# Local-attention transformer stack: queries scaled before their transposes, maximum subtracted in the score banks, one exponential per chunk, scores and weighing in halves

## The reference, cut to what matters

```
qkv = x @ Wqkv                              # 128 -> 3 * 16 heads * 64
q = l2norm(q) * q_scale;  k = l2norm(k) * k_scale
q, k = rotary(q), rotary(k)                 # times cos, plus rotated half times sin, xpos scales
# windows of 32 queries, each sees its own and the previous 32 keys, causal
sim = einsum('bhwie,bhwje->bhwij', bq, bk2) * 8.0
sim = where(mask, -max, sim)
attn = softmax(sim, -1)
out = einsum('bhwij,bhwje->bhwie', attn, bv2) @ Wo
```

## Time and profile before

| | |
|---|---|
| median of three runs | 3912.69 us |
| profiled execution, its own time | 3949.71 us |
| its span | 3947.9 us |
| mean granted TensorE clock | 0.962 |
| TensorE matmul busy | 3373.5 us (85%) |
| ScalarE busy | 3201.0 us (81%) |
| VectorE busy | 2676.7 us (68%) |
| GpSimd busy | 2370.0 us (60%) |

### The profile page before, as it was taken

One profiled execution on the slowest core, in us unless ns is written; L12 is line 12 of the kernel. 1 busy time (PEld: TensorE's weight loads), 2 busy tenths in 40 slices (PEclk: granted clock), 3 DMA queues, 4 the chain that ended last, 5 costly groups with the idle time before them and its releaser, 6 DMA issues.

```text
span 3947.9 us, 154738 instructions
## 1 busy us (share of the span) xinstructions
PE 3373.5 (85%) x64080; PEld 2589.6 (66%) x64080; DVE 2676.7 (68%) x5196; ACT 3201.0 (81%) x5968; POOL 2370.0 (60%) x1960
## 2 busy tenths in 40 slices
PE   6888888888888888887677888889888888888886
PEld 4666766766676667665335667667666667667664
DVE  4776777776666776765446666777766767777675
ACT  5898888888888888886227888888888888898883
POOL 5676666666666666663006666666666666666661
PEclk8999999999999999999778999999999999999998
DMA  2232232232232232232002322332232232232221
GB/s 82 75 83 69 74 81 72 75 78 72 71 83 68 70 86 64 76 80 58 6 0 61 80 69 70 77 79 70 75 80 71 74 77 75 75 77 69 69 64 34
DMA packets 207434, 272.84 MB, mean 69 GB/s; under 512 B 55700, under 2 KB 101648, under 8 KB 206736
## 3 DMA queue, kind: packets, MB, share of 16 engines
q1 hardware_dynamic: 206736, 262.94, 26.3%
HBM read 60.35 MB, written 1.05 MB: 16 GB/s over the span
## 4 chain that ended last, share of the span: by engine, by line
PE 62%; ACT 20%; issue 13%; DVE 2%; SPq 1%; POOL 1%; DMA 0%; DVEq 0%; ACTq 0%; POOLq 0%
PE PS L329 16%; ACT PR L728 9%; PE PS L377 6%; PE PS L439 5%; PE PS L486 5%; PE PS L378 5%; PE PS L379 5%; PE PS L495 5%; PE PS L463 5%; PE PS L521 3%; PE PS L431 2%; ACT PT L737 1%; ACT OT L756 1%; ACT L728 1%; ACT VS L749 1%
## 5 line engine op out<-in xcount | busy, mean ns | idle before, releaser
L1176 POOL TENSOR_TENSOR V<-RAWQK,TAB 128x512 f32<-128x512 f32 x768 | 971.3, 1287 | 936.1 <-PE PS L329 660.2
L728 ACT ACTIVATE PR<-PS,NB,RN 128x64 f32<-128x64 f32 x3072 | 930.6, 449 | 3.4 <-DVE NB L959 2.8
L377 PE MATMUL PS<-WH,XH 128*128 128x512 f32 x1152 | 519.3, 451 | 36.0 <-POOL XL L1158 24.1
L463 PE MATMUL PS<-V,PT 64*32 64x64 f32 x24576 | 344.9, 226 | 224.3 <-issue 223.8
L329 PE MATMUL PS<-EYE,V 128*128 128x128 f32 x3072 | 413.9, 279 | 92.3 <-ACT PR L728 91.5
L378 PE MATMUL PS<-WH,XL 128*128 128x512 f32 x1152 | 472.8, 410 | 2.5 <-issue 2.5
L379 PE MATMUL PS<-WL,XH 128*128 128x512 f32 x1152 | 472.4, 410 | 1.7 <-issue 1.7
L463 PEld LDWEIGHTS PS<-V,PT 64*32 64x32 f32 x24576 | 281.5, 106 | 286.9 <-issue 282.7
L1209 POOL TENSOR_TENSOR V<-V,U 128x1024 f32<-128x1024 f32 x192 | 453.6, 2362 | 14.9
L1202 POOL TENSOR_TENSOR V<-V,U 128x1024 f32<-128x1024 f32 x192 | 454.8, 2369 | 0.0
L329 PEld LDWEIGHTS PS<-EYE,V 128*128 128x128 f32 x3072 | 359.4, 143 | 136.0 <-issue 107.7
(11 more groups left out here) (150 smaller groups left out, 6913.6 us busy)
## 6 DMA issues: line engine op xcount, KB each, us to landing
V<-VS SPq DMA_DIRECT2D x3072, 64.0 KB
ROTB<-c_rot SPq DMA_DIRECT2D x192, 128.0 KB, 2.4
WSTAGE<-wqkv SPq DMA_DIRECT2D x33, 512.0 KB, 3.8
WO<-wo SPq DMA_DIRECT2D x12, 512.0 KB, 3.8
W<-w SPq DMA_DIRECT2D x12, 341.0 KB, 3.1
QKS<-qks SPq DMA_DIRECT2D x12, 128.0 KB, 3.7
W<-w SPq DMA_DIRECT2D x12, 114.0 KB
VS<-wqkv SPq DMA_DIRECT2D x2, 512.0 KB, 4.2
```

The source lines that it names most:

```text
L377: pe.matmul(o, XH[:, p, :], WH[:, w, cols], start=True, stop=False)
L463: mm = pe.matmul(PS[WIN * w:WIN * (w + 1), B_O + r, j * DH:(j + 1) * DH], PT[DH * r:DH * (r + 1), j, WIN * w:WIN * (w + 1)], V2[DH * r:DH ...
L728: ins = act.activation(PR[:, 2 * j + r, :], PS[:, B_S + r, j * 2 * WIN:(j + 1) * 2 * WIN], ACT.Exp, bias=NB[:, c % 2, h:h + 1], scale=RN[: ...
L1176: ins = pool.tensor_tensor(paired(V[:, k])[:, :, :, h * half:(h + 1) * half], split(RAWQK[:, k])[:, :, :, (1 - h) * half:(2 - h) * half], ...
```

## The change

Queries get a step of their own on GpSimd, `scale_queries`, a product with the reciprocal norm ahead of their transposes. `row_max` then takes the maximum and subtracts it within the score banks, and a single exponential reads both banks. Scores and weighing are each split into two steps, one per `r`, with a semaphore each; the mask matmul of a bank goes with its half. The order of each engine's steps, the turns between them and the PSUM banks are set anew. The diff, cut to its core (the waits for `scored` and `weighed` become waits for both halves in every place; `after(...)` lines name the readers of the new banks):

```diff
-B_Q = 3
-B_K = 5
-B_V = 1
-B_TQ = 5
+B_Q = 5
+B_K = 3
+B_V = 3
+B_TQ = 0
 B_TK = 3
-B_S = 5
-B_P = 2
-B_O = 0
-B_TO = 2
+B_S = 0
+B_O = 5
+B_P = 3
+B_TO = 5
 B_WO = 2
-B_F1 = 0
-B_F2 = 1
-B_F3 = 4
-LAG, CHAIN_OFF, CHAINS = 7, 1, 107
+B_F1 = 2
+B_F2 = 0
+B_F3 = 1
+LAG, CHAIN_OFF, CHAINS = 7, 0, 106
...
                 def turn_queries(c):
-                    pe.wait_ge(q_turned, count(inv, c))
+                    pe.wait_ge(q_scaled, count(inv, c))
...
-                def scores(c):
+                def score_half(c, r):
+                    pe.matmul(PS[:, B_S + r, :], EYEB[:, :], rep(MASK[:, 1 if c % CH == 0 else 0, :], [P, NP_, 2 * WIN], 1),
+                              start=True, stop=False, skip_group_check=True)
                     pe.wait_ge(q_kept, count(inv, c))
                     pe.wait_ge(k_kept, count(inv, c))
                     held(halo_kept, count(inv, c - 1))
                     for j in range(NP_):
                         for w in range(NW):
-                            for r in range(2):
-                                mm = pe.matmul(PS[WIN * w:WIN * (w + 1), B_S + r, j * 2 * WIN:(j + 1) * 2 * WIN],
...
+                            mm = pe.matmul(PS[WIN * w:WIN * (w + 1), B_S + r, j * 2 * WIN:(j + 1) * 2 * WIN],
+                                           QT[DH * r:DH * (r + 1), j, WIN * w:WIN * (w + 1)],
+                                           KT[DH * r:DH * (r + 1), j, WIN * w:WIN * (w + 2)],
+                                           start=False, stop=True, skip_group_check=True)
+                    mm.then_inc(scored[r], 1)
...
+                def weigh_half(c, r):
                     for j in range(NP_):
                         for w in range(NW):
+                            mm = pe.matmul(PS[WIN * w:WIN * (w + 1), B_O + r, j * DH:(j + 1) * DH],
+                                           PT[DH * r:DH * (r + 1), j, WIN * w:WIN * (w + 1)],
+                                           V2[DH * r:DH * (r + 1), c % 2, w, j * DH:(j + 1) * DH],
+                                           start=True, stop=True, skip_group_check=True)
+                    mm.then_inc(weighed[r], 1)
...
-                for t in range(108):
+                for t in range(107):
+                    queries(t - 1)
                     turn_weights(t - 3)
-                    ffn_third(t - 2)
-                    scores(t - 2)
-                    turn_outputs(t - 4)
-                    weigh(t - 3)
-                    queries(t)
-                    project_out(t - 4)
-                    turn_queries(t - 1)
+                    turn_queries(t - 2)
+                    ffn_first(t - 1)
+                    turn_keys(t - 2)
+                    ffn_third(t - 1)
+                    ffn_second(t - 1)
+                    weigh_a(t - 3)
+                    weigh_b(t - 3)
                     values(t - 1)
+                    turn_outputs(t - 3)
+                    scores_a(t - 2)
+                    scores_b(t - 2)
                     keys(t)
-                    turn_keys(t - 1)
-                    ffn_first(t - 1)
-                    ffn_second(t - 1)
+                    project_out(t - 3)
...
                 def exponentials(c):
-                    act.wait_ge(bias_done, count(inv, c))
+                    act.wait_ge(shifted, count(inv, c))
-                    for r in range(2):
-                        for j in range(NP_):
-                            h = r * NP_ + j
-                            ins = act.activation(PR[:, 2 * j + r, :], PS[:, B_S + r, j * 2 * WIN:(j + 1) * 2 * WIN], ACT.Exp,
-                                                 bias=NB[:, c % 2, h:h + 1], scale=RN[:, c % 2, h:h + 1])
-                    ins.then_inc(exp_done, 1)
+                    act.activation(PR[:, :, :].rearrange("p (j r) k -> p r j k", r=2),
+                                   rows(B_S).rearrange("p r (j k) -> p r j k", k=2 * WIN), ACT.Exp).then_inc(exp_done, 1)
...
-                for t in range(108):
+                for t in range(107):
+                    keep_halo(t - 3)
                     copy_keys(t - 1)
+                    exponentials(t - 3)
+                    square_keys(t - 1)
+                    copy_queries(t - 1)
+                    keep_weights(t - 3)
+                    keep_queries(t - 2)
+                    ffn_early(t - 1)
+                    square_queries(t - 1)
                     keep_keys(t - 2)
...
+                    ffn_late(t - 1)
                     shift(t)
...
                     keep_values(t - 1)
+                    keep_outputs(t - 3)
...
                 def row_max(c):
+                    s = rows(B_S).rearrange("p b (j k) -> p b j k", k=2 * WIN)
+                    dve.tensor_reduce(MX[:, :, :], s, AX.X, ALU.max)
                     dve.drain()
-                    dve.scalar_tensor_tensor(NB[:, c % 2, :], MX[:, :], -1.0, RN[:, c % 2, 0:HEADS],
-                                             ALU.mult, ALU.mult).then_inc(bias_done, 1)
+                    dve.tensor_tensor(s, s, rep(MX[:, :, :], [P, 2, NP_, 2 * WIN], 3), ALU.subtract).then_inc(shifted, 1)
...
                 for t in range(111):
-                    add_back(t - 4)
+                    scale_outputs(t - 3)
+                    norm(t - 1)
+                    row_max(t - 2)
+                    cos_keys(t)
+                    add_back(t - 3)
                     scale_keys(t - 1)
+                    row_sum(t - 2)
                     cos_queries(t)
+                    sum_keys(t)
                     sum_queries(t)
...
+                    ffn(t)
...
+                def scale_queries(c):
+                    pool.wait_ge(norms, chain_count(inv, c))
+                    pool.wait_ge(q_turned, count(inv, c))
+                    rn = RN[:, c % 2, 0:HEADS].rearrange("p (r j) -> p j r", r=2).unsqueeze(3).broadcast_to([P, NP_, 2, DH])
+                    v = V[:, 0].rearrange("p (j r) d -> p j r d", r=2)
+                    pool.tensor_tensor(v, v, rn, ALU.mult).then_inc(q_scaled, 1)
...
-                for t in range(108):
-                    sin_queries(t - 2)
-                    sin_keys(t - 2)
-                    add_queries(t - 2)
+                for t in range(107):
+                    table(t)
                     low_part(t - 1)
                     add_keys(t - 2)
-                    table(t)
-                    ffn(t - 2)
+                    scale_queries(t - 2)
+                    ffn(t - 1)
+                    sin_queries(t - 1)
+                    add_queries(t - 1)
+                    sin_keys(t - 1)
```

More of the change, by code:

```diff
@@ L454, in weigh, with weigh_a @@
+                def weigh_a(c):
                     if not live(c):
                         return
[L456 to L459, removed]
-                    for j in range(NP_):
[L461 to L466, removed]
@@ L467, in weigh, with weigh_b @@
-                    mm.then_inc(weighed, 1)
+                    after(use(uq_done, c + 2), use(o_kept, c - 1), use(o_scaled, c - 1))
+                    weigh_half(c, 0)
+                def weigh_b(c):
+                    if not live(c):
+                        return
+                    after(use(uq_done, c + 2), use(o_kept, c - 1), use(o_scaled, c - 1))
+                    weigh_half(c, 1)
                 def turn_outputs(c):
@@ L483, in project_out @@
                     pe.wait_ge(o_kept, count(inv, c))
-                    after(use(o_kept, c), use(p_kept, c + 1), use(v_kept, c + 2), use(xb_done, c - 1))
+                    after(first(c + 2), use(xb_done, c - 1), first(c + 0), first(c - 1))
                     for h in range(NP_):
@@ L500, in ffn_first @@
                         return
-                    after(use(o_scaled, n - 2), first(n - 1), first(n - 2), first(n - 3))
+                    after(use(xb_done, n - 3), first(n - 1), first(n - 2), first(n - 3))
                     if q == 0:
@@ L524, in ffn_second @@
                         return
[L525 removed]
+                    after(use(q_kept, n - 1), use(exp_done, n - 2), second(n - 1), second(n - 2), second(n - 3))
                     hidden(g, 1 if q == 2 else 4, B_F2)
@@ L531, in ffn_third @@
                         return
-                    after(use(k_kept, n), use(uq_done, n + 1), third(n - 1), third(n - 2), third(n - 3))
+                    after(use(q_kept, n - 1), use(exp_done, n - 2), third(n - 1), third(n - 2), third(n - 3))
                     if q == 0:
@@ L704, in keep_keys @@
                     act.wait_ge(k_rows, count(inv, c))
-                    held(scored, count(inv, c - 1))
+                    for half in scored:
+                        held(half, count(inv, c - 1))
                     held(halo_kept, count(inv, c - 1))
@@ L973, in scale_outputs @@
                     dve.drain()
-                    dve.wait_ge(weighed, count(inv, c))
+                    for half in weighed:
+                        dve.wait_ge(half, count(inv, c))
```

(3 more changed lines are left out.)

96 lines of the change are left out of this document (40 added, 56 removed).

## The result

The changed kernel takes 3798.61 us (median of four runs, 3792.71 to 3810.15) against 3916.6 us for the kernel before on the same occasion: a ratio of 0.9702, with a 95% interval of 0.9673 to 0.9732. It is 3% faster; the forecast was 3817 us. The profiled execution took 3810.15 us.

What follows compares the result with a forecast made beforehand. No engine is full; TensorE leads the chain of waits (62%) in a turn of 18.48 us. Terms -0.55 - 0.30 - 0.15 + 0.50 = -0.50 us a chunk, times 192 = -96: 3912.7 - 96 = 3817 us, range 3680 to 4020.

Steps and rivals of the forecast that it cites:

- Exponential, -0.55: ScalarE: one 1.1 us exponential for sixteen ends TensorE's 91.5 us wait and returns some clock; -0.55 us a chunk, bounds 0 and 1.25.
- VectorE: Subtraction added within the score banks, 1.22 us; net +1.0 us a chunk, 13.9 us busy becomes 14.9.
- GpSimd: Scaling of the queries ahead of their transposes, 2.37 us (above, 2.6); hidden, with 3 us to spare.
- Tiled stages, 4.90 to 4.60: Scores and weighing on TensorE: 2.0 + 2.0 + 0.3 + 0.3 = 4.6 us a chunk for 4.90, -0.30.
- the hole: TensorE's "issue" idle in the dense scores and weighing, instructions used faster than blocks arrive; 1.45 us a chunk becomes 0.3.
- tile changes: TensorE goes from full array to tiles and back six times a turn, not four; 0.15 us each, +0.3.
- The half-clock stretch: Weighing before the change at granted clock 0.50: 13.9 ns a record with 8 tiles, taken for 4 tiles at full clock.
- Rival A: Each half of scores and weighing keeps its row group's pace, 20 ns a record: about 4065 us; chance 0.13.
- rival D: Weight loads of one row group don't overlap: 15.4 us for 2.8, +12.6 us a chunk, about 6300 us; chance 0.02.
- Place of the output transposes and new waits, -0.15 + 0.50: TensorE: output transposes follow values, not scores, -0.15 us a chunk; new waits on VectorE and ScalarE +0.5, bounds 0.1 and 1.5.
- The clock: Mean granted clock, 0.962 before, expected at or over that; a tenth of the 150 us not granted was counted as gain.
- Filling and emptying, under 10 us: One turn of the loop fewer in each stack only shortens the emptying, under 10 us; not counted in the sum.

Runs made afterwards that it cites:

- the joined form: Changed kernel with scores and weighing each in one step again, row groups alternating, both masks ahead: 0.9375 of the kernel before.
- the one with both stages joined: Changed kernel with scores and weighing each in one step, and row maximum and subtraction left out: 0.9372 of the kernel before.

## Why the prediction was right

*What bounds the turn.* Right: TensorE, with the rest behind it. It is busy 93% now, and taking 363 us from GpSimd, or in the joined form 469 from VectorE, changes nothing.

*Exponential, -0.55.* Right in mechanism, sized too low: alone in the old order it measured 0.69 a chunk, the clock with it (0.962 to 0.970). The single instruction is 1.03 us for 1.1.

*VectorE.* The subtraction is 1.23 us for 1.22. It is hidden, as costed; the run that shows it is the one with both stages joined.

*GpSimd.* Hidden, as costed. The price was too high: 1.94 us, below the lower of my two rows (2.37). A sum of the same size was no good row for a product with a broadcast factor.

*Tiled stages, 4.90 to 4.60.* The number came out, 4.60, but not its split. The pace is right, 14 ns a record for 13.9, and so is the hole, 0.33 us for 0.3. The two stages themselves are busy 4.27 us where I had 4.0, and the 0.3 for tile changes, which I had counted within the 4.60, comes on top. The sum compared two measures: 4.90 is busy and idle time by groups, in which the stages before are 3.45 us busy, while 2.0 + 2.0 is read from start to start at full clock, where they were 3.0; and the one more tail that I gave scores is not in its 2.0. That 4.60 was met is luck. The split mask alone is busy 36 us longer than the 114.2 before:

```profile
L424 PE MATMUL PS<-MASK,EYEB 128*128 128x512 bf16 x384 | 150.1, 391 | 0.0
```

The half-clock stretch gave the pace of four tiles at full clock. Rival A (20 ns) and rival D are out. By the strict reading of the Trainium skill, "TensorE: Matmul & The Clock Gate", Part 3, where a weight load overlaps matmuls only if the row group differs, the 64 records of a half, at 0.06 us each, would have taken an estimated 3.8 us or more. This case's trace does not agree: they take 1.10. (The price of D started from 2.8 us for two stages that the forecast has at 4.0; that makes it no less out.)

What the sum did not say is what the halves are worth by themselves. I weighed them together with the hole, against the old order, and a -0.30 came out that reads like a gain of the halves. The gain in idle time was mostly the order's. Against the joined form in the same order the halves cost 0.69 us a chunk in the stages, 3.4% of the time in all.

*Place of the output transposes and new waits, -0.15 + 0.50.* The waits are small: 14.6 us for the scaled outputs, 17.7 for the exponentials by the matmul rows, 67.3 and 39.3 by those of the weight loads. Here they are:

```profile
PEld PS L328 <- DVE ON L988: 67.3, 167, 1.6
...
PEld PS L328 <- ACT PR L739: 39.3, 48, 2.0
...
PE PS L328 <- ACT PR L739: 17.7, 47, 1.8
...
PE PS L328 <- DVE ON L988: 14.6, 36, 1.5
```

Even by the loads that is 0.55 us a chunk, by the matmuls 0.17, so 0.50 was at the upper end. The place is as said: the transposes of the outputs go from 1.06 to 0.90 us where nothing holds them.

*The clock.* I wrote that it would be at or over 0.962; it is 0.960 in the profiled execution and 0.960 to 0.964 over the runs, so it did not rise. The exponential alone raised it to 0.970 in the old order; with the halves of weighing in the new order it is down again, and with weighing joined it is 0.975.

*Filling and emptying, under 10 us.* Too low: 27 us of the span's 140 lie outside the turns. Inside them -0.60 us a turn stand against -0.50, but 0.13 of it may be the 25 us by which the two profiled executions lie apart from their medians. So far as two executions tell, the turn came out about as forecast, and most of the miss is the filling, which was left out of the sum.

So 96 us were forecast and 118 measured. Per turn the terms that moved are the exponential (0.14 more gain), the waits (some 0.3 less loss) and the tiled stages with their tile changes (some 0.3 more loss); they nearly cancel. The mechanisms of the exponential and of the hole are shown by runs; that the time came within half a per cent is in good part this luck.

## What to carry to other kernels

When a change bundles an order with a form of the work, price each form also against its alternative in the new order, not only the bundle against the old kernel: here one part (halves) cost 3.4% inside a change that gained 3%, and the version without it runs at 0.9375. Here small tiled matmuls were better off with all eight tiles in turn (10 ns a record) than with four (14 ns), even though the slower form halved the hole. In this kernel the order closed more of the hole, and for nothing; I take it that work with few instructions between two dense stages does that. And compare a stretch at half clock with one at full clock: with four tiles the time per record nearly doubled (14 to 27 ns), with eight it rose by less (10 to 13.3), so with eight something besides the array's clock held the pace at full clock.

## What the runs showed of the hardware

- Four tiles of 64 rows by 32 columns, two records per fp32 matmul of 64 columns: 14 ns a record at full clock, 27 at half clock. In this timeline of the changed kernel the first half of the scores begins at granted clock 0.50; the clock comes back about two thirds into it, and the second half has the full clock:

```profile
2208.34 1.60 PE L431 MATMUL PS<-KT,QT 64*32 64x64 f32 x64
2209.88 0.39 PE L424 MATMUL PS<-MASK,EYEB 128*128 128x512 bf16 x1
2210.20 1.10 PE L431 MATMUL PS<-KT,QT 64*32 64x64 f32 x64
```

```profile
2208.40:2209.40 1.00, 1.00 (x41) 1.00 (x44) 0.00 (x0) 0.64 (x1) 1.00 (x1) 0.50 0.48 121
2209.40:2209.60 0.20, 0.20 (x23) 0.20 (x16) 0.00 (x0) 0.00 (x0) 0.20 (x1) 0.85 0.19 52
```

  The first 40 records start between 2208.34 and 2209.40, 27 ns a record: four of them every 0.107 us. At full clock four start every 0.056 us. With eight tiles it is eight records in the same 0.107 us at half clock, 13.3 ns a record, and a mean of 10 ns at full clock.
- A scale read from SBUF adds 89 ns to an activation of 64 columns in such a burst, a bias another 90 (123, 212, 302 ns).
- Dense stages of small matmuls idle TensorE at the borders of instruction blocks: 99% of the distances between the holes before are multiples of 125.4 matmul records. The idle time hangs on how fast the instructions are used (278.0 us at 10 ns a record, 120.6 at 14, in one order) and on what lies between the stages (278.0 and 131.9 us).
- On GpSimd a 128x1024 product with a broadcast factor takes 1.94 us in place, a sum of the same size 2.37.
- In the new order the mean granted clock with weighing in halves is 0.960 and 0.963, with weighing joined 0.975 (0.959 to 0.967 against 0.968 to 0.976 over all runs of these kernels). Why is left open.
